# A macaron block on one core: the first tile of each stage turned ahead of the last quarter of the product before it, and the places of the small pieces laid anew

## The chip, the cores and the metric

One Trainium2 chip, one NeuronCore of it. The metric is the device time of one execution in microseconds; lower is better. The numbers given for a kernel are the median of several executions.

## The reference

The input is a 2 x 2048 x 256 float32 tensor, 4096 tokens of 256 values. Three residual blocks follow each other:

```
x = x + 0.5 * moe(layernorm(x))
x = x + recurrence(layernorm(x))
x = x + 0.5 * moe(layernorm(x))

def moe(x):                       # 8 experts, one per token
    probs = softmax(x @ Wr + br); e = argmax(probs)
    h = relu(layernorm_g_b(x) @ W1[e] + b1[e])      # 256 -> 1024
    return (h @ W2[e] + b2[e]) * max(probs)         # 1024 -> 256

def recurrence(x):                # 3 layers of width 64
    x = x @ down.T
    for l in range(3):
        xc = conv4(x) + cb        # causal, 4 taps
        r, i = sigmoid(xc @ Wr[l].T + rb), sigmoid(xc @ Wi[l].T + ib)
        a = exp(8 * r * log_sigmoid(log_a[l]))
        h_t = a_t * h_(t-1) + sqrt(1 - a_t^2) * i_t * xc_t
        x = rms_norm(h @ Wo[l].T) * nw[l]
    return x @ up.T
```

The expert of a token is data: the rows are sorted by expert on the chip.

## The kernel before, in words

**Routing and tiles.** Each of the two expert layers is a pass (pass 0 and pass 1). For a chunk `c` of the tokens (four chunks of 1024 tokens, 512 of each sequence), the router's logits, the choice of the expert, its rank among the rows of that expert and the row's place are computed (`choose`, `place`, `keep_counts` on VectorE, `logits`, `turn_logits`, `ranks`, `counts` on TensorE), and GpSimd (POOL) writes every row into a DRAM table sorted by expert (`route`, L633, two indirect DMAs of 128 rows each time). `tables` on VectorE (six parts) then works out which rows of the table each tile of 128 rows takes and which expert it has; its part 4 raises `s_tab`.

A tile (slot) goes through this chain: SP fetches its 128 rows (`slot_rows`, L465) and the 1 MB first weights of its expert (`slot_weights`, L472), VectorE normalises it (`norm`, L1163), TensorE turns it with two transposes (`turn_input`, L1678), ScalarE applies gain and bias (`affine`, L1417), TensorE multiplies by the first weights (`first_product`, four quarters q of 8 matmuls of 128x128, L1691), ScalarE and VectorE add the bias and clip, a half each (`activate`, L1427 and L1172), TensorE multiplies by the second weights (`second_product`, four quarters of 4 matmuls of 256 columns, L1705), VectorE reads the product and adds the bias (L1181) and finishes the row (L1188, both in `finish`), POOL stores it at its token's place (`store`, L642). 37 tiles are used in each pass; 32 of them in straight code.

**The steady order on TensorE.** In the place of slot i (`fixed_slot`): turn tile i + 1, the four quarters of the first product of tile i, the four quarters of the second product of tile i - 1. `second_product` of tile i waits in its first quarter for both activations and for `m_yk`, VectorE's reading of the product of tile i - 1.

**Stages.** A pass can't begin with all tiles: a tile needs the chunks that its rows come from to be routed. So the tiles come in stages, `FIRST[0] = [0, 9]` and `FIRST[1] = [0, 4, 13, 21]`. Before a stage SP waits (`next_rows`, L481) until the tables of the stage are ready and all rows of its chunks have landed in DRAM, and fetches the first tile only then. On TensorE the turn of the stage's first tile can't stand in the slot before (`next_input` leaves it out), and `begin_stage` (L1723) makes a place of its own for the stage: it turns tile i, then runs the second product of tile i - 1, with pieces of other work between the quarters. After it `fixed_slot` goes on with `next_input`, the turn of tile i + 1, and the first product of tile i. On VectorE `begin_stage` (L1191) does `finish(i - 2)`, the pieces of the place, then `norm(i)` and `norm(i + 1)`; `finish(i - 1)` comes behind these.

**Pieces beside the tiles.** The recurrence, its layernorm and the routing of later chunks are cut into pieces, and every piece of every engine has a number, its place, in the lists at the head of the file. `PLACE[p][i]` is the place of slot i, one more for each stage start before it; `beside(at)` in each engine's block runs the pieces whose number k lies in the stretch `24 * at` to `24 * at + 23`. TensorE has eight such stretches in a place (one behind each quarter), so its place is k / 192; the other engines have two (before and after `activate`, or before and after GpSimd's wait for the half-way point of the first product, `half_through`), so theirs is k / 48. Tile 9 of pass 0 has place 10, its `begin_stage` place 9; in pass 1 tiles 0, 4, 13 and 21 have places 41, 46, 56 and 65, their `begin_stage` the place before. For a chunk c and a layer l of the recurrence the pieces follow in this order: `spread` (PE), `rescale` (DVE), `tap` (ACT), `convolve` (DVE), `gates` (PE), `TANH` (ACT), `gate_input` (DVE), `root` (ACT), `scan` (DVE), `project` (PE), `squares` (ACT), `norms` (PE), `rms_root` (ACT), `inverse` (DVE); each waits on a semaphore of the one before. In front of layer 0 stand the layernorm's moments (DVE), its power (POOL), `transposes` and `logits` (L1548) and `down` (L1585) on TensorE, and `wide` (DVE), which waits for the power.

TensorE also has `in_motion`, matmuls without use before its first real work.

## Time and profile before

| | us |
|---|---|
| median of 3 executions | 715.09 (714.1 to 717.19) |
| the profiled execution, its device time | 712.98 |
| its span, from the first to the last instruction | 711.2 |
| TensorE matmuls busy in it | 657.6 (92%) |
| VectorE busy | 409.6 (58%) |
| ScalarE busy | 272.2 (38%) |
| GpSimd busy | 171.9 (24%) |

Times in the rows below are microseconds from the span's start unless marked ns. PE is TensorE, PEld its weight load, DVE VectorE, ACT ScalarE, POOL GpSimd, SPq the DMA issues of SyncE. A bracket at the end of a row of the timeline is the idle time of the engine before that group and what ended it. Matmul ends are modelled, so that groups which follow each other overlap a little.

### The profile page before, as it was taken

How to read it: one execution, taken by the hardware profiler on the slowest of the kernel's cores; microseconds unless marked ns; L12 is line 12 of the kernel's file. 1: busy time of each engine (PE TensorE's matmuls, PEld its weight loads, DVE VectorE, ACT ScalarE, POOL GpSimd, SP SyncE). 2: the span in 40 equal slices, each digit the busy share in tenths (PEclk: the TensorE clock that was granted, in tenths of full speed). 3: DMA queues.
4: the chain of work that ended last, by engine and by line, in shares of the span. 5: the costliest groups of instructions: out<-in, count | busy, mean ns of one | idle time of the engine just before them, and what ended most of it. 6: DMA issues, size and time to landing. Idle time of an engine off the chain costs nothing.

```text
span 711.2 us, 15531 instructions
## 1 busy us (share of the span) xinstructions
PE 657.6 (92%) x4420; PEld 576.9 (81%) x4420; DVE 409.6 (58%) x1427; ACT 272.2 (38%) x642; POOL 171.9 (24%) x177
## 2 busy tenths in 40 slices
PE   7639997999999999999998989999899989999993
PEld 5429996999988878798777868889689979999992
DVE  7746772333346577776887767787567623333331
ACT  3214221322245557544663436654443223222220
POOL 4733433111121120123302340124212511111111
PEclk9659999999999999999999989999999999999997
DMA  9979673955554463336316345423464466453530
GB/s 281 324 259 396 202 246 109 324 173 193 173 207 142 155 202 117 121 129 217 130 54 238 108 178 208 149 83 120 152 236 141 143 231 207 152 197 101 178 124 14
DMA packets 59920, 126.51 MB, mean 178 GB/s; under 512 B 8106, under 2 KB 36661, under 8 KB 59701
## 3 DMA queue, kind: packets, MB, share of 16 engines
q1 hardware_dynamic: 53204, 108.50, 45.7%
q0 software_dynamic: 6624, 16.92, 6.5%
q8 instruction: 42, 0.69, 0.4%
q14 instruction: 50, 0.40, 0.2%
HBM read 106.36 MB, written 20.35 MB: 178 GB/s over the span
## 4 chain that ended last, share of the span: by engine, by line
PE 70%; DVE 12%; issue 6%; DVEq 5%; DMA 3%; POOL 2%; ACT 1%; POOLq 0%; SPq 0%; ACTq 0%
PE bank L1691 31%; PE bank L1705 29%; PE bank L1678 2%; DVE st L746 2%; POOL routed_rows L633 1%; PE bank L1595 1%; DVEq L400 1%; PE bank L1602 1%; DMA pay<-routed_rows 1%; DVE rec L1082 1%; DVE rec L1058 1%; PE bank L1628 1%; PE bank L1607 1%; PE bank L1533 1%; DVE act_t L1172 1%
## 5 line engine op out<-in xcount | busy, mean ns | idle before, releaser
L1691 PE MATMUL bank<-mn_t,w 128*128 128x128 f32 x2368 | 284.7, 277 | 0.6 <-DVE act_t L1172 0.5
L1691 PEld LDWEIGHTS bank<-mn_t,w 128*128 128x128 f32 x2368 | 275.0, 193 | 9.5 <-issue 7.7
L1705 PE MATMUL bank<-w,act_t 128*128 x1184 | 278.0, 386 | 2.9 <-issue 2.0
L1705 PEld LDWEIGHTS bank<-w,act_t 128*128 128x128 f32 x1184 | 220.7, 193 | 39.5 <-issue 12.8
L1417 ACT ACTIVATE mn_t<-bank,vec 128x128 f32<-128x128 f32 x152 | 61.2, 453 | 236.3 <-PE bank L1678 236.3
L1172 DVE TENSOR_SCALAR act_t<-bank,vec 128x128 f32<-128x128 f32 x296 | 83.3, 344 | 101.9 <-PE bank L1691 88.7
L1427 ACT ACTIVATE act_t<-bank,vec 128x128 f32<-128x128 f32 x296 | 84.6, 368 | 76.0 <-PE bank L1691 75.8
L1181 DVE TENSOR_TENSOR y_b<-bank,b_all 128x256 f32<-128x256 f32 x74 | 31.4, 425 | 104.7 <-PE bank L1705 93.1
L642 POOL DMA_INDIRECT x_middle<-res,pay x37 | 37.2, 1007 | 219.6 <-DVE res L1188 182.7
L642 POOL DMA_INDIRECT out_x<-res,pay x37 | 36.4, 984 | 204.6 <-DVE res L1188 150.2
L633 POOL DMA_INDIRECT routed_rows<-rows,dest x64 | 64.1, 1001 | 53.6 <-PE bank L1691 25.5
L1678 PE MATMUL bank<-ident,mn 128*128 128x128 f32 x152 | 30.4, 282 | 21.6 <-DVE mn L1163 12.8
L1163 DVE TENSOR_SCALAR mn<-pay 128x256 f32<-128x256 f32 x78 | 31.9, 409 | 25.3 <-DMA pay<-routed_rows 24.5
L1678 PEld LDWEIGHTS bank<-ident,mn 128*128 128x128 f32 x152 | 20.5, 145 | 31.6 <-DVE mn L1163 14.2
L625 POOL TENSOR_TENSOR inv_std<-var_eps,minus_half 128x16 f32<-128x16 f32 (+1 forms) x12 | 31.3, 2610 | 51.7 <-DVE var_eps L756 37.3
L1188 DVE SCALAR_TENSOR_TENSOR res<-y_b,pay 128x256 f32<-128x256 f32 x74 | 35.8, 484 | 7.2 <-issue 0.2
L746 DVE BATCH_NORM_STATS2 st<-rows 128x6 f32<-128x256 f32 x96 | 33.7, 414 | 2.6 <-DMA rows<-in_L_attn_h 0.7
L1058 DVE SCALAR_TENSOR_TENSOR rec<-seq,lay,rec 128x512 f32<-128x512 f32 x36 | 27.0, 749 | 2.0 <-issue 0.2
L1321 ACT ACTIVATE xn_t<-bank 128x512 f32<-128x512 f32 x32 | 17.8, 599 | 19.8 <-PE bank L1533 19.6
L1533 PE MATMUL bank<-ident,rows 128*128 128x128 f32 x128 | 20.6, 316 | 0.0
L1533 PEld LDWEIGHTS bank<-ident,rows 128*128 128x128 f32 x128 | 17.7, 166 | 3.1 <-issue 2.2
L1359 ACT ACTIVATE rec<-bank,lay 64x512 f32<-64x512 f32 x24 | 16.4, 682 | 9.0 <-PE bank L1595 8.8
(212 smaller groups left out, 456.5 us busy)
## 6 DMA issues: line engine op xcount, KB each, us to landing
w<-in_L_ffn_W SPq DMA_DIRECT2D x82, 1024.0 KB, 5.2
pay<-routed_rows SPq DMA_DIRECT2D x78, 130.0 KB, 2.1
rows<-in_L_attn_h SPq DMA_DIRECT2D x8, 512.0 KB, 7.2
rows<-x_middle SPq DMA_DIRECT2D x8, 512.0 KB, 5.0
routed_rows<-fill SPq DMA_DIRECT2D x2, 1040.0 KB, 7.7
routed_rows<-rows,dest POOLq DMA_INDIRECT x64, 2.7
b_all<-in_L_ffn_b SPq DMA_DIRECT2D x1, 1024.0 KB, 12.1
x_middle<-res,pay POOLq DMA_INDIRECT x37, 2.5
```

Of the source, the lines that this page charges most:

```text
L633: g.indirect_dma_start(out=routed[f], out_offset=bass.IndirectOffsetOnAxis(ap=dest[:, t:t + 1], axis=0), in_=rows[:, t * RW:(t + 1) * RW], ...
L642: g.indirect_dma_start(out=x_out if p else x_mid, out_offset=bass.IndirectOffsetOnAxis(ap=pay[p][i % RING][:, C_ID:C_ID + 1].bitcast(I32), ...
L746: v.bn_stats(st[:, jj * 6:jj * 6 + 6], tile_of(c, b, j, 0, D))
L1058: last = v.scalar_tensor_tensor(out=r_x_b[cc], in0=seq[:, k:k + CH], scalar=unit(l, k), in1=r_x_b[cc], op0=ALU.mult, op1=ALU.add)
L1172: last = v.tensor_scalar(act_t[i % 2][:, c * P:(c + 1) * P], b_hid[1][:, c % 4 * P:(c % 4 + 1) * P], vec[:, ds(eb + c, 1)], 0.0, ALU.add, ...
L1188: v.scalar_tensor_tensor(out=res[p][i % 2][:, :], in0=y_b[i % 2][:, :], scalar=a[:, C_GATE:C_GATE + 1], in1=a[:, 0:D], op0=ALU.mult, op1=A ...
L1417: last = a.activation(mn_t[p][i % 2][:, k * P:(k + 1) * P], b_in[i % 2][:, k * P:(k + 1) * P], ACT.Identity, scale=vec[:, V_G + k:V_G + k ...
L1427: last = a.activation(act_t[i % 2][:, c * P:(c + 1) * P], b_hid[0][:, c * P:(c + 1) * P], ACT.Relu, bias=vec[:, ds(eb + c, 1)])
L1533: last = t.transpose(bk[cc][n % 2][:, j * P:(j + 1) * P], tile_of(c, b, j, k * P, P), ident[:, :])
L1678: last = t.transpose(b_in[i % 2][:, k * P:(k + 1) * P], mn[p][i % 2][:, k * P:(k + 1) * P], ident[:, :])
L1691: last = t.matmul(b_hid[half][:, c % 4 * P:(c % 4 + 1) * P], w1[i % W1S][:, k * F + c * P:k * F + (c + 1) * P], mn_t[p][i % 2][:, k * P:(k ...
L1705: last = t.matmul(b_out[i % 2], act_t[i % 2][:, c * P:(c + 1) * P], w2[:, ds(eb * (WE // FC) + c * D, D)], start=c == 0, stop=c == FC - 1)
```

## The change

In `begin_stage` of TensorE the wait for the tables and the turn of the stage's first tile move from in front of the whole second product of tile i - 1 to in front of its last quarter (for i = 0 there is no tile before it, and nothing moves). With it the places in the lists were laid anew. GpSimd's lists, LN_POW, R_POW and R_SCATTER, are the same number for number. The places that differ most lie in these stretches: the routing of chunk 3 in pass 0 (choose, ranks, place, counts about half a place to one place earlier), and in pass 1 everything of chunk 3's layernorm and of layers 1 and 2 of chunks 2 and 3 between places 42 and 55.

```diff
--- before.py
+++ after.py
@@ -21,52 +21,52 @@
 
 SUB = 24
 LN_POW = [984, 1272, 1705, 2161]
-LN_WIDE = [1008, 1296, 1704, 2160]
-LN_LOGITS = [4081, 5161, 6865, 8472]
-LN_KEEP_LOGITS = [1033, 1276, 1707, 2136]
-DOWN = [4080, 5162, 6864, 8473]
-KEEP_DOWN = [1032, 1278, 1706, 2160]
-LN_MOMENTS = [[984, 985], [1272, 1273], [1680, 1681], [2114, 2115]]
-LN_TRANSPOSE = [[3984, 4032], [5089, 5113], [6672, 6720], [8257, 8424]]
-LN_KEEP = [[984, 1008], [1273, 1275], [1657, 1704], [2088, 2112]]
-UP = [[5760, 5856], [7057, 7104], [9528, 9600], [11112, 11184]]
-ADD = [[1443, 1465], [1776, 1800], [2380, 2401], [2784, 2786]]
-SPREAD = [[4104, 5163, 6912, 8641], [4656, 5736, 8064, 9504], [5160, 6480, 8880, 10344]]
-RESCALE = [[1032, 1299, 1730, 2209], [1153, 1440, 2016, 2377], [1297, 1632, 2210, 2592]]
-TAP = [[1034, 1320, 1752, 2232], [1176, 1440, 2016, 2379], [1277, 1656, 2233, 2592]]
-CONVOLVE = [[1033, 1300, 1752, 2211], [1176, 1442, 2040, 2378], [1298, 1656, 2256, 2594]]
-GATES = [[4248, 5328, 7056, 9048], [4800, 5832, 8256, 9552], [5232, 6673, 9144, 10488]]
-TANH = [[1080, 1322, 1755, 2280], [1200, 1464, 2064, 2381], [1321, 1658, 2281, 2640]]
-GATE_INPUT = [[1080, 1344, 1778, 2281], [1224, 1489, 2113, 2425], [1320, 1705, 2304, 2688]]
-ROOT = [[1104, 1368, 1920, 2328], [1224, 1512, 2137, 2448], [1392, 1705, 2329, 2712]]
-SCAN = [[1104, 1392, 1824, 2328], [1248, 1560, 2116, 2520], [1416, 1729, 2352, 2736]]
-PROJECT = [[4560, 5664, 7392, 9432], [5088, 6336, 8616, 10224], [5713, 6960, 9481, 11040]]
-SQUARES = [[1128, 1416, 1921, 2376], [1272, 1608, 2161, 2544], [1418, 1753, 2378, 2760]]
-NORMS = [[4608, 5712, 7440, 9480], [5112, 6384, 8640, 10272], [5737, 7008, 9505, 11088]]
-RMS_ROOT = [[1152, 1417, 1922, 2377], [1274, 1609, 2162, 2568], [1419, 1754, 2380, 2761]]
-INVERSE = [[1152, 1417, 1969, 2376], [1274, 1608, 2208, 2570], [1441, 1753, 2379, 2760]]
+LN_WIDE = [1008, 1297, 1704, 2161]
+LN_LOGITS = [4081, 5161, 6865, 8424]
+LN_KEEP_LOGITS = [1033, 1276, 1707, 2112]
+DOWN = [4080, 5162, 6864, 8425]
+KEEP_DOWN = [1032, 1278, 1706, 2114]
+LN_MOMENTS = [[984, 985], [1272, 1273], [1680, 1681], [2065, 2137]]
+LN_TRANSPOSE = [[3984, 4032], [5089, 5113], [6672, 6720], [8232, 8257]]
+LN_KEEP = [[984, 1008], [1273, 1275], [1657, 1704], [2040, 2088]]
+UP = [[5760, 5856], [7057, 7104], [9482, 9504], [11112, 11184]]
+ADD = [[1443, 1465], [1776, 1800], [2377, 2381], [2784, 2786]]
+SPREAD = [[4104, 5163, 6912, 8689], [4656, 5736, 8064, 9505], [5160, 6480, 8688, 10416]]
+RESCALE = [[1032, 1299, 1730, 2208], [1153, 1440, 2016, 2380], [1296, 1632, 2162, 2592]]
+TAP = [[1034, 1320, 1752, 2208], [1176, 1440, 2016, 2380], [1277, 1656, 2162, 2640]]
+CONVOLVE = [[1033, 1300, 1752, 2256], [1176, 1442, 2041, 2401], [1298, 1656, 2209, 2616]]
+GATES = [[4248, 5328, 7056, 9096], [4800, 5832, 8256, 9720], [5208, 6673, 9024, 10560]]
+TANH = [[1080, 1322, 1755, 2280], [1200, 1464, 2064, 2424], [1321, 1658, 2256, 2641]]
+GATE_INPUT = [[1080, 1344, 1778, 2304], [1224, 1489, 2088, 2448], [1320, 1705, 2280, 2688]]
+ROOT = [[1104, 1368, 1920, 2329], [1224, 1512, 2113, 2472], [1392, 1705, 2328, 2712]]
+SCAN = [[1104, 1392, 1824, 2352], [1248, 1560, 2114, 2497], [1416, 1729, 2328, 2736]]
+PROJECT = [[4560, 5664, 7392, 9481], [5088, 6336, 8520, 10104], [5713, 6960, 9432, 11040]]
+SQUARES = [[1128, 1416, 1921, 2378], [1272, 1608, 2160, 2544], [1418, 1753, 2376, 2760]]
+NORMS = [[4608, 5712, 7440, 9483], [5112, 6384, 8568, 10224], [5737, 7008, 9480, 11088]]
+RMS_ROOT = [[1152, 1417, 1922, 2379], [1274, 1609, 2161, 2568], [1419, 1754, 2377, 2761]]
+INVERSE = [[1152, 1417, 1969, 2378], [1274, 1608, 2160, 2570], [1441, 1753, 2376, 2760]]
 R_POW = [[None, None, 0, 48], [1512, 1848, 2424, 2808]]
-R_CHOOSE = [[None, None, 3, 96], [1512, 1968, 2448, 2832]]
-R_EXP = [[None, None, 49, 120], [1560, 1992, 2472, 2856]]
-R_RANKS = [[None, None, 216, 552], [6192, 7944, 9936, 11472]]
-R_PLACE = [[None, None, 48, 144], [1536, 2017, 2472, 2856]]
-R_COUNTS = [[None, None, 288, 696], [6288, 8160, 10008, 11544]]
-R_KEEP_COUNTS = [[None, None, 73, 168], [1561, 2041, 2496, 2880]]
+R_CHOOSE = [[None, None, 2, 72], [1512, 1968, 2424, 2832]]
+R_EXP = [[None, None, 48, 96], [1560, 1992, 2425, 2856]]
+R_RANKS = [[None, None, 193, 408], [6192, 7944, 9816, 11472]]
+R_PLACE = [[None, None, 48, 96], [1536, 2017, 2472, 2856]]
+R_COUNTS = [[None, None, 264, 504], [6288, 8160, 9984, 11544]]
+R_KEEP_COUNTS = [[None, None, 50, 121], [1561, 2040, 2496, 2880]]
 R1_TRANSPOSE = [0, 48]
-R1_KEEP = [1, 24]
+R1_KEEP = [0, 24]
 R1_LOGITS = 192
-R1_KEEP_LOGITS = 48
-R_TURN_LOGITS = [[None, None, None, 217], [5952, 7368, 9696, 11256]]
-R_MOMENTS = [[[None, None], [None, None], [None, None], [1, 2]], [[1464, 1488], [1777, 1825], [2400, 2424], [2785,
+R1_KEEP_LOGITS = 49
+R_TURN_LOGITS = [[None, None, None, 216], [5952, 7368, 9600, 11256]]
+R_MOMENTS = [[[None, None], [None, None], [None, None], [0, 1]], [[1464, 1488], [1777, 1825], [2379, 2400], [2785,
     2808]]]
 R_SCATTER = [[[None, None, None, None], [None, None, None, None], [72, 120, 168, 216], [264, 312, 360, 408]],
     [[1560, 1608, 1656, 1704], [2040, 2088, 2136, 2160], [2472, 2520, 2568, 2616], [2856, 2904, 2952, 3000]]]
-TABLE_PARTS = [[[None, None, None, None, None, None], [169, 192, 240, 264, 288, None]], [[1584, 1609, 1633, 1682,
-    1683, 1728], [2064, 2065, 2088, 2089, 2112, 2280], [2497, 2544, 2568, 2569, 2593, 2616], [2881, 2904, 2905,
+TABLE_PARTS = [[[None, None, None, None, None, None], [168, 216, 217, 264, 312, None]], [[1584, 1609, 1633, 1682,
+    1683, 1728], [2064, 2066, 2112, 2113, 2115, 2136], [2520, 2521, 2544, 2545, 2568, 2569], [2881, 2904, 2905,
     2952, 2953, None]]]
-LAYER_COLUMNS = 0
-EXP_LOG_A = 0
-LOG_SIGMOID = 72
+LAYER_COLUMNS = 49
+EXP_LOG_A = 72
+LOG_SIGMOID = 120
 
 
 
@@ -1723,11 +1723,16 @@
             def begin_stage(p, i):
 
                 beside(8 * (PLACE[p][i] - 1))
-                pe.wait_ge(s_tab, tables_at(p, FIRST[p].index(i)))
-                turn_input(p, i)
-                if i:
+                if i == 0:
+                    pe.wait_ge(s_tab, tables_at(p, 0))
+                    turn_input(p, i)
+                else:
                     eb = second_expert(p, i - 1)
                     for q in range(4):
+                        if q == 3:
+
+                            pe.wait_ge(s_tab, tables_at(p, FIRST[p].index(i)))
+                            turn_input(p, i)
                         second_product(p, i - 1, q, eb)
                         beside(8 * (PLACE[p][i] - 1) + 1 + q)
 
```

## Rows read from the trace of the kernel before

**Rows 1.** The page: busy time (share) and instructions; one group of part 5.

```profile
PE 657.6 (92%) x4420; PEld 576.9 (81%) x4420; DVE 409.6 (58%) x1427; ACT 272.2 (38%) x642; POOL 171.9 (24%) x177
...
L1058 DVE SCALAR_TENSOR_TENSOR rec<-seq,lay,rec 128x512 f32<-128x512 f32 x36 | 27.0, 749 | 2.0 <-issue 0.2
```

**Rows 2.** TensorE's waits over the span: us in total, times, longest.

```profile
PE bank L1678 <- DVE mn L1163: 12.8, 2, 11.2
PE bank L1678 <- issue: 6.7, 3, 3.3
...
PE bank L1602 <- DVE rec L1082: 2.0, 4, 0.7
...
PE bank L1595 <- DVE rec L1058: 1.5, 3, 0.6
```

**Rows 3.** Timeline around tile 9 of pass 0: start, us, engine, line, operation.

```profile
114.68 3.62 PE L1705 MATMUL bank<-w,act_t 128*128 x16
...
115.25 0.97 POOL L633 DMA_INDIRECT routed_rows<-rows,dest  x1 [0.30 <-issue]
...
121.14 0.34 SPq L465 DMA_DIRECT2D pay<-routed_rows  x1
...
121.56 0.41 PE L1678 MATMUL bank<-ident,mn 128*128 128x128 f32 x2 [3.26 <-issue]
...
122.72 5.40 PE L1705 MATMUL bank<-w,act_t 128*128 x16 [0.75 <-issue]
...
126.02 0.41 DVE L1163 TENSOR_SCALAR mn<-pay 128x256 f32<-128x256 f32 x1 [4.49 <-DMA pay<-routed_rows]
...
128.18 2.06 PE L1691 MATMUL bank<-mn_t,w 128*128 128x128 f32 x17
```

**Rows 4.** Stretches: window, us, PE busy (groups), granted clock, DMA share, GB/s.

```profile
123.00:128.00 5.00, 5.00 (x17) 0.66 1.02 409
420.00:428.00 8.00, 7.79 (x28) 0.57 0.97 361
576.00:581.00 5.00, 2.96 (x14) 1.00 1.03 392
```

**Rows 5.** Timeline around tile 4 of pass 1.

```profile
406.96 1.95 PE L1691 MATMUL bank<-mn_t,w 128*128 128x128 f32 x16
...
408.84 1.07 PE L1548 MATMUL bank<-xn_t,wr_c 128*32 128x512 f32 x8
...
409.83 1.94 PE L1585 MATMUL bank<-xn_t,down_t 128*64 128x512 f32 x8
...
414.11 0.97 POOL L633 DMA_INDIRECT routed_rows<-rows,dest  x1 [0.30 <-issue]
...
415.89 2.04 POOL L625 TENSOR_TENSOR inv_std<-var_eps,minus_half 128x8 f32<-128x8 f32 x1 [0.81 <-DVE var_eps L754]
...
417.49 0.35 SPq L465 DMA_DIRECT2D pay<-routed_rows  x1
...
420.21 1.51 PE L1607 MATMUL bank<-half_sel,rec 128*128 128x2 f32 x8 [1.26 <-ACT rec L1374]
...
422.89 5.87 PE L1705 MATMUL bank<-w,act_t 128*128 x16
...
424.10 0.41 DVE L1163 TENSOR_SCALAR mn<-pay 128x256 f32<-128x256 f32 x1 [2.38 <-DMA pay<-routed_rows]
...
428.82 2.84 PE L1691 MATMUL bank<-mn_t,w 128*128 128x128 f32 x24
```

**Rows 6.** Timeline around tile 13 of pass 1.

```profile
508.99 0.42 DVE L1181 TENSOR_TENSOR y_b<-bank,b_all 128x256 f32<-128x256 f32 x1 [1.15 <-PE bank L1705]
...
514.17 0.41 DVE L1163 TENSOR_SCALAR mn<-pay 128x256 f32<-128x256 f32 x1 [3.72 <-DMA pay<-routed_rows]
...
515.06 3.74 PE L1691 MATMUL bank<-mn_t,w 128*128 128x128 f32 x32
```

**Rows 7.** Timeline around tile 21 of pass 1.

```profile
578.74 0.41 PE L1678 MATMUL bank<-ident,mn 128*128 128x128 f32 x2 [1.57 <-issue]
...
579.25 0.81 ACT L1417 ACTIVATE mn_t<-bank,vec 128x128 f32<-128x128 f32 x2 [6.06 <-PE bank L1678]
...
583.38 3.74 PE L1691 MATMUL bank<-mn_t,w 128*128 128x128 f32 x32
```

## The prediction, made before the changed kernel was run

> **What bounds the kernel now.** I read the page first: TensorE is busy for 92% of the span [rows 1], so what can be won is its idle time and its slow clock. Then its waits: outside the loading of the first tiles, nearly all idle time stands in front of one line, L1678, the turning of an input tile; the waits that the recurrence pieces cause are small beside it, 2.0 us for the projections and 1.5 us for the gates over the whole kernel [rows 2]. Of L1678's waits, the 12.8 us are those of the very first tile and of tile 0 of the second pass, which the new `begin_stage` handles as the old did. The change can reach the four other stage starts: tile 9 of pass 0 and tiles 4, 13 and 21 of pass 1. For each I read the timeline of all engines, and asked two things: when the first tile of the stage is normalised (that releases the turn), and when the second is, because `next_input` turns the second tile before the first tile's first product may start. That second tile is the one a plain reading of the diff forgets.
>
> **Pass 0, tile 9.** The product in front (tile 7's, L1705 at 114.68 for 3.62 us) ends at 118.30. The last routed rows were issued at 115.25, the tile could be fetched only when they had landed, and the turn comes at 121.56 after 3.26 us of idling, and only then tile 8's 16 matmuls run, at 122.72 for 5.40 us; the first product of tile 9 starts at 128.18 [rows 3]. After the change 12 of those 16 fill the wait. They can't start at 118.30: `second_product` waits until VectorE has read the product before it, and at a stage start that reading begins 0.46 us after the product's end and takes 0.42 us (at tile 13 product 11 ends at 508.53 and the reading starts at 508.99 [rows 6]), so about 119.2. Twelve matmuls at 0.217 us (16 in about 3.5 us) end at 121.8, the turn takes 0.2, the last four 0.9: 122.9. But tile 10, fetched at 121.14, is normalised at 126.02 to 126.43, because its rows and 1 MB of weights come over the same queue [rows 3]. TensorE waits again, from 122.9 to 126.5, and starts the first product at 126.8 for 128.18: 1.4 us won, not 3.3.
>
> The clock takes it back. In the trace the granted clock falls after the wait: 0.66 on average in 123 to 128, which is 0.34 x 5 / 0.5 = 3.4 us at half of 2.4 GHz, the other of its two levels being 1.2; a stretch without a fall, 576 to 581, has 1.00 [rows 4]. It cost half of 3.4, 1.7 us, of which a part was free since tile 10 was late anyway. After the change 3.6 us of idling lie in one piece, directly in front of slots in which nothing waits, and I expect the same fall there, now paid in full: +1.7. Sum of this start: -1.4 + 1.7 = +0.3 us. Its bounds: -1.4 if the clock holds, +2.0 if it falls twice.
>
> **Pass 1, tile 4.** Here most of the re-placed pieces meet. In the old order logits and down projection of chunk 3 (408.84 to 411.77, 2.9 us) stand inside tile 3's first product; projection and norms of layer 1, chunk 2 stand behind tile 2's second product, where TensorE waits 1.26 us for ScalarE until 420.21; the clock is low for 0.43 x 8 / 0.5 = 6.9 us [rows 4], and tile 3's 16 matmuls take 5.87 us. First product of tile 4: 428.82 [rows 5]. In the new order logits and down stand before tile 3's first product, project behind its last quarter (PROJECT 8616 to 8520), norms inside tile 2's second product (8640 to 8568). Take H as the moment when tile 3's first product is half through: 408.75 before (406.96 with 1.95 us, less the overlap), and 2.9 us later after. POOL's list is not changed in one number, so its last four row DMAs still wait for H, at 0.97 and a gap of 0.30 us each (the last began at 414.11, SP went on at 417.49 [rows 5], 2.4 us after that one's end). Before, a store was in their way; after, the later H leaves the store in front. So SP fetches tile 4 at H + 0.1 + 5.0 + 2.4 = H + 7.5. Tile 5 was normalised 6.6 us behind that fetch, at 424.10 [rows 5], plus 0.41: H + 14.6. TensorE's own chain: first product's rest 1.8 (as its first half), second product 3.5, wait for the read 0.9, twelve matmuls 2.6, and project, norms and the pair of spreads (the layer-2 spread stands here now) at 1 us each, my estimate from the norms' 1.51 us in the low clock, 3.0: H + 11.8, turn of tile 4, last quarter until H + 12.9, wait for tile 5 until 14.6, first product at H + 14.9. Against 428.82 = old H + 20.1, and with H 2.9 later and 0.5 us of spread brought forward: 20.1 - 14.9 - 2.9 + 0.5 = 2.8, and I take -2.7. Covers: VectorE does inverse, wide and rescale before it normalises tile 4; at no more than the 0.75 us each of its costliest 128x512 form [rows 1] these are 2.2 us, beside eight matmuls and two spreads; if that cover is gone, the turn is late by up to 1 us, but tile 5's wait hides it. Table part 5, moved from behind the stage's start to before it, adds seven short instructions to VectorE in the same cover. Bounds: -4.4 (tile 5 as soon as TensorE is free) to +0.7 (the 3.4 us of low clock, twice 1.7, come back).
>
> **Pass 1, tile 13.** Product 11 is read at 508.99 + 0.42, tile 14 normalised at 514.17 to 514.58, first product at 515.06 [rows 6]. The second tile again binds: 0.2 us. The layer-2 spread of chunk 3 now stands behind the half-way point that releases POOL, so the rows come 0.5 us earlier against TensorE's work: together -0.7. The gates of chunk 3 now stand before product 12 and wait for a convolution that begins after tile 12's activation; TensorE then idles some 0.3 us there, which the 1.8 us wait for tile 14 would have taken anyway: nothing. If the clock falls, +1.7: bounds -0.7 and +1.0.
>
> **Pass 1, tile 21.** The rows are there; TensorE waited 1.57 us for VectorE to finish product 19 first [rows 7]. After: start at 577.17 + 0.9 = 578.05, twelve matmuls to 580.65; turn, affine of ScalarE ready 1.3 us after the turn's start (578.74 to 579.25 + 0.81 [rows 7]), so tile 22 is turned at 582.0 and the first product starts at 582.3 for 583.38: -1.1. The price of the change, the affine that now hides behind four matmuls instead of sixteen, is in it: 0.5 us. Bounds -1.2 and -0.6.
>
> **All other places.** The pieces of early chunk 3 (routing of pass 0) and of the recurrence move, but each is issued once as before. What they can win is the 3.5 us of [rows 2] at most, of which little lies outside tile 4's stage; what they can lose is of the same size. I take 0, bounds -1.5 and +2.
>
> **Sum.** +0.3 - 2.7 - 0.7 - 1.1 = -4.2 us. Against the profiled execution's own 712.98 us that is 708.8. That execution was 2.1 us faster than the median of the runs shown, 715.09, so 710.9 us is my number for the median.
>
> A rule against the change stands in the Trainium skill, "TensorE: Matmul & The Clock Gate", section "HAM oscillation — how this bites in real kernels": short bursts of matmuls between DMA waits make the clock fall again at every burst. This trace agrees in part: it fell at tile 9 after one wait of 3.26 us, but also at tile 4 where no single wait was over 1.3 us [rows 5], and not at tile 21 after 1.57 us [rows 4, 7].
>
> **The rivals.** (A) The waits only move and the clock falls there: the second tile binds at tiles 4, 9 and 13, and each new wait (3.6, 1.7, 1.8 us in one piece) is followed by a half-clock stretch. For it: tile 9. Against: at tile 21 1.57 us did no harm. Price: 1.7 us at each of tiles 4 and 13 over the forecast, -0.8 us in all: 714.3. By the skill's rule it would be this one. Chance 0.32. (B) Slower: VectorE's queue at tile 4. Tile 4 is normalised only behind inverse, wide and rescale, wide needs POOL's power after the four row DMAs, rescale needs TensorE's spread between the quarters. If the power is late, TensorE stands in the spread, then in the turn, and then in tile 5. It decides once the power ends over 2.5 us after product 3 could have started; with both waits and two clock stretches that is 3 to 6 us instead of -2.7, and with A's falls the kernel ends near 719. Against it: POOL's power took 2.04 us from 415.89 [rows 5] and was over before tile 4's turn even in the old order. Chance 0.08. (C) All of it: the clock holds at tile 9 too and the re-placed pieces save 1 to 2 us: 707.5 to 709.5. Chance 0.15. (D) The change doesn't do what it says, because the first tile was never last: that is true of tile 21 alone, where the gain is VectorE's order, and is in the sum.
>
> **Numbers.** Forecast 0.45 (709.5 to 712.5), A 0.32, C 0.15, B 0.08. A measurement of this kernel can tell about 0.5%, 3.6 us, from no change. Under 711.5: all of C and two thirds of the forecast, 0.45 with rounding; A, the rest of the forecast and some of B are no change, 0.47; slower 0.08. The range leaves out half of C's low end and B: 708.0 to 715.0.
>
> **What would show it.** Right: L1678's idle time falls from four waits to waits in front of the second tiles, ended by tile rows; 12 L1705 matmuls directly before each first turn, 4 behind; tile 9's first product about 8.5 us after product 7's end; the wait at L1607 gone; one low stretch near 125 and none near 421. Wrong: idle time at L1595, L1602 or L1617 above 5 us, or low stretches at tiles 4 and 13 (A), or a wait of over 2 us in front of tile 4's turn (B).

## The result and the profile after

The changed kernel takes 718.44 us (median of 20 executions, 714.53 to 721.34) against 715.12 us for the kernel before (20 executions, 713.3 to 718.26): a ratio of 1.0039 by all executions, 95% interval 1.0025 to 1.0052 (the quotient of the two medians is 1.0046). It is 0.4% slower. The forecast was 710.9 us with a range of 708.0 to 715.0; the result lies outside it. The profiled execution took 719.86 us with a span of 718.1, 1.4 us over its median, while the one before lay 2.1 us under its own. So the two spans differ by 6.9 us, of which about half is the choice of executions. One correction to the counts ahead of this section: a float32 matmul of the code stands as two records in the trace (the first product issues 16 and has 32 records), so where the kernel's description and the prediction count the matmuls of a product or of a quarter (16, 12, 8 or 4), these are records (a transpose stands as one); the times are not touched by that, and what follows counts records.

The page, and TensorE's waits (us in total, times, longest), which answer to [rows 1, 2]:

```profile
PE 662.8 (92%) x4420; PEld 580.7 (81%) x4420; DVE 409.8 (57%) x1427; ACT 270.1 (38%) x640; POOL 172.8 (24%) x177
```

```profile
PE bank L1678 <- DVE mn L1163: 8.2, 4, 3.1
PE bank L1705 <- DVE y_b L1181: 6.4, 6, 2.2
...
PE bank L1691 <- ACT act_t L1427: 1.9, 1, 1.9
```

The waits `L1678 <- issue`, 6.7 us before, are gone: the first tile of a stage no longer keeps TensorE waiting. In their place stand the normalising of the second tile, VectorE's reading of a product (L1705, up to 2.2 us) and a wait for ScalarE's activation that was not there. Of the 8.2 us of normalising, 1.6 us in front of tile 1 of pass 1 were there before; the new ones are 3.10 us at tile 10, 3.15 us at tile 14 and 0.39 us at tile 5. The 11.2 us of the very first tile [rows 2] stand at another line in this profile, so the totals of this group can't be compared.

The timeline of the changed kernel in pass 0 (start, us, engine, line, operation), which answers to [rows 3]:

```profile
75.66 0.16 DVE L1023 TENSOR_SCALAR logs<-logs 128x3 f32<-128x3 f32 x1
...
79.91 0.42 DVE L1181 TENSOR_TENSOR y_b<-bank,b_all 128x256 f32<-128x256 f32 x1 [0.82 <-issue]
...
80.58 3.72 PE L1705 MATMUL bank<-w,act_t 128*128 x16 [0.90 <-DVE y_b L1181]
...
89.30 0.21 DVE L917 TENSOR_TENSOR_SCAN seg_end<-seg_n,zero_e 128x32 f32<-128x32 f32 x1
...
95.48 0.42 DVE L1181 TENSOR_TENSOR y_b<-bank,b_all 128x256 f32<-128x256 f32 x1
...
117.77 3.62 PE L1705 MATMUL bank<-w,act_t 128*128 x16
...
122.21 2.85 PE L1705 MATMUL bank<-w,act_t 128*128 x12 [0.82 <-DVE y_b L1181]
...
128.77 0.41 DVE L1163 TENSOR_SCALAR mn<-pay 128x256 f32<-128x256 f32 x1 [4.50 <-DMA pay<-routed_rows]
...
129.24 0.44 PE L1678 MATMUL bank<-ident,mn 128*128 128x128 f32 x2 [3.10 <-DVE mn L1163]
...
129.52 5.37 PE L1691 MATMUL bank<-mn_t,w 128*128 128x128 f32 x32
```

And in pass 1, around tiles 3, 4 and 5, then tile 13 ([rows 5, 6]):

```profile
415.18 3.84 PE L1691 MATMUL bank<-mn_t,w 128*128 128x128 f32 x32
...
423.04 1.41 DVE L746 BATCH_NORM_STATS2 st<-rows 128x6 f32<-128x256 f32 x4
...
425.74 0.42 DVE L1181 TENSOR_TENSOR y_b<-bank,b_all 128x256 f32<-128x256 f32 x1 [0.59 <-issue]
...
426.41 3.40 PE L1705 MATMUL bank<-w,act_t 128*128 x8 [2.18 <-DVE y_b L1181]
...
433.61 3.74 PE L1691 MATMUL bank<-mn_t,w 128*128 128x128 f32 x32
...
436.10 0.41 DVE L1163 TENSOR_SCALAR mn<-pay 128x256 f32<-128x256 f32 x1 [1.46 <-DMA pay<-routed_rows]
...
436.50 0.68 DVE L1103 TENSOR_TENSOR seq<-rec,bank 128x512 f32<-128x512 f32 x1
...
437.22 0.82 ACT L1350 ACTIVATE rec<-seq,lay 128x512 f32<-128x512 f32 x1 [2.59 <-DVE seq L1103]
...
438.17 1.15 ACT L1427 ACTIVATE act_t<-bank,vec 128x128 f32<-128x128 f32 x4
...
439.46 1.13 PE L1691 MATMUL bank<-mn_t,w 128*128 128x128 f32 x8 [1.89 <-ACT act_t L1427]
...
508.46 0.48 DVE L1188 SCALAR_TENSOR_TENSOR res<-y_b,pay 128x256 f32<-128x256 f32 x1
...
509.22 0.97 POOL L642 DMA_INDIRECT out_x<-res,pay  x1 [4.28 <-DVE res L1188]
...
510.50 0.98 POOL L633 DMA_INDIRECT routed_rows<-rows,dest  x1 [0.31 <-issue]
...
515.48 0.34 SPq L465 DMA_DIRECT2D pay<-routed_rows  x1
...
522.40 0.69 PE L1678 MATMUL bank<-ident,mn 128*128 128x128 f32 x2 [3.15 <-DVE mn L1163]
...
522.89 5.13 PE L1691 MATMUL bank<-mn_t,w 128*128 128x128 f32 x32
```

Stretches of the changed kernel with a low clock around its stages (window, us, PE busy, granted clock, DMA share, GB/s), which answer to [rows 4]:

```profile
125.00:134.00 9.00, 5.90 (x35) 0.81 1.00 398
388.00:395.00 7.00, 6.28 (x43) 0.76 0.48 144
426.00:431.00 5.00, 4.59 (x17) 0.66 0.77 267
437.00:446.00 9.00, 7.11 (x49) 0.81 0.46 156
522.00:528.00 6.00, 5.59 (x36) 0.72 0.88 343
```

**Where the time went.** I took from each timeline the start of every tile's first product (the L1691 group; other line numbers in the experiments) and subtracted. "1.4" is tile 4 of pass 1. The row `e9` belongs to a kernel described below.

| us from ... to ... | before | after | e1 | e2 | e3 | e9 |
|---|---|---|---|---|---|---|
| span's start to 0.8 | 111.1 | 114.2 | 111.0 | 114.0 | 111.2 | 111.1 |
| 0.8 to 0.10 (start of the stage of tile 9) | 20.9 | 20.7 | 20.6 | 21.3 | 20.8 | 16.2 |
| 0.10 to 1.0 | 253.4 | 254.0 | 253.3 | 253.3 | 254.0 | 254.1 |
| 1.0 to 1.1 | 3.9 | 5.5 | 5.5 | 3.9 | 5.4 | 5.2 |
| 1.1 to 1.4 | 39.6 | 39.1 | 38.7 | 39.6 | 39.0 | 38.4 |
| 1.4 to 1.6 | 14.6 | 17.2 | 14.6 | 14.6 | 17.2 | 14.6 |
| 1.6 to 1.20 (with tile 13) | 126.5 | 127.2 | 126.7 | 126.3 | 127.0 | 126.3 |
| 1.20 to 1.21 | 13.4 | 12.4 | 12.4 | 13.4 | 12.4 | 12.4 |
| 1.21 to the end | 127.8 | 127.8 | 127.8 | 127.8 | 127.8 | 127.8 |
| span | 711.2 | 718.1 | 710.5 | 714.2 | 714.6 | 705.9 |

What was aimed at moved little: tile 9 -0.1, tile 4 -0.5, tile 21 -1.0. Three places that I had priced at nothing lost more: the routing in pass 0 (+3.1), the stretch behind tile 4 (+2.5) and 1.0 to 1.1 (+1.6).

Each column is one profiled execution, and some rows move by themselves. Thirteen profiles of this document have the old places of pass 0 and the same code until tile 8; they take 111.0 to 113.5 us for it, 111.9 in the mean. Above that mean the changed kernel and e2 (114.2 and 114.0) lie by 2.1 to 2.3 us, not by 3.1. The stretch 1.4 to 1.6 has a spread as well: the changed kernel and e3 take 17.2 us there, but e5, e6, e11 and e14, whose pieces in front of tile 4's activation are the same, 14.9 to 15.4. So the sizes are taken from the ratios of many executions below, and the rows say where.

### The profile page after: what moved, and what is told of

Same layout as the page of the kernel before. It is cut to its first block, busy times and chain, and to the rows that moved or that the text cites. A ratio compares the mean times of both kernels' runs of the same rounds, so it can differ in the third digit from the quotient of the medians.

```text
span 718.1 us, 15529 instructions
## 1 busy us (share of the span) xinstructions
PE 662.8 (92%) x4420; PEld 580.7 (81%) x4420; DVE 409.8 (57%) x1427; ACT 270.1 (38%) x640; POOL 172.8 (24%) x177
## 4 chain that ended last, share of the span: by engine, by line
PE 71%; issue 7%; DMA 6%; DVE 5%; POOL 2%; another core or an unknown queue 2%; DVEq 2%; SPq 1%; ACT 1%; POOLq 0%; ACTq 0%
PE bank L1691 31%; PE bank L1705 27%; DMA pay<-routed_rows 4%; PE bank L1678 2%; PE bank L1533 2%; POOL routed_rows L633 2%; PE bank L1595 2%; PE bank L1602 1%; DMA routed_rows<-rows,dest 1%; DVE st L746 1%; PE bank L1628 1%; PE bank L1607 1%; PE bank L1585 1%; PE bank L1561 1%
## 5 line engine op out<-in xcount | busy, mean ns | idle before, releaser
L1691 PE MATMUL bank<-mn_t,w 128*128 128x128 f32 x2368 | 289.3, 280 | 2.2 <-ACT act_t L1427 1.9
L1691 PEld LDWEIGHTS bank<-mn_t,w 128*128 128x128 f32 x2368 | 279.7, 196 | 10.5 <-issue 10.3
L1705 PE MATMUL bank<-w,act_t 128*128 x1184 | 275.7, 383 | 6.6 <-DVE y_b L1181 6.4
L1705 PEld LDWEIGHTS bank<-w,act_t 128*128 128x128 f32 x1184 | 218.4, 191 | 43.3 <-issue 17.5
L1678 PE MATMUL bank<-ident,mn 128*128 128x128 f32 x152 | 30.4, 283 | 10.6 <-DVE mn L1163 8.2
L1678 PEld LDWEIGHTS bank<-ident,mn 128*128 128x128 f32 x152 | 20.3, 145 | 21.2 <-DVE mn L1163 10.5
L1561 PEld LDWEIGHTS bank<-pick,lg_t 128*128 128x128 f32 x64 | 9.1, 217 | 14.3 <-ACT lg_t L1330 14.0
L1533 PE MATMUL bank<-ident,rows 128*128 128x128 f32 x128 | 20.6, 313 | 0.0
L1561 PE MATMUL bank<-pick,lg_t 128*128 128x16 f32 x64 | 9.2, 278 | 12.3 <-ACT lg_t L1330 12.3
```

The costliest lines, as they stand in the source:

```text
L1533: last = t.transpose(bk[cc][n % 2][:, j * P:(j + 1) * P], tile_of(c, b, j, k * P, P), ident[:, :])
L1678: last = t.transpose(b_in[i % 2][:, k * P:(k + 1) * P], mn[p][i % 2][:, k * P:(k + 1) * P], ident[:, :])
L1691: last = t.matmul(b_hid[half][:, c % 4 * P:(c % 4 + 1) * P], w1[i % W1S][:, k * F + c * P:k * F + (c + 1) * P], mn_t[p][i % 2][:, k * P:(k ...
L1705: last = t.matmul(b_out[i % 2], act_t[i % 2][:, c * P:(c + 1) * P], w2[:, ds(eb * (WE // FC) + c * D, D)], start=c == 0, stop=c == FC - 1)
```

## The experiments

The theory when they were planned: the turn itself wins, and the new numbers in the lists lose more. The rival: the turn loses, by waits and clock falls at the second tiles (A of the prediction). The kernels of one group shared their runs of the kernel before, whose medians were 716.24 (e1 to e4), 715.18 (e5 to e8), 715.66 (e9 to e12) and 716.77 us (e13 to e15). The lines of the experiments are shifted: the turn L1678, the first product L1691, the second L1705 and SP's fetch L465 stand at L1674, L1687, L1701 and L461, in e7, e9 and e15 at L1683, L1696, L1710 and L461.

### e1, e2, e3 and e12: the change in halves

e1 has the new `begin_stage` and every old place; e12 is e1 again, in another group.

```diff
-                pe.wait_ge(s_tab, tables_at(p, FIRST[p].index(i)))
-                turn_input(p, i)
-                if i:
+                if i == 0:
...
+                        if q == 3:
+                            pe.wait_ge(s_tab, tables_at(p, FIRST[p].index(i)))
+                            turn_input(p, i)
```

> The new begin_stage with every place of the kernel before. Theory P (the places): the turn itself wins and the new places lose. It should be 1 to 3 us faster than before (712 to 714 against 715.1), tile 21 by about 1.0 us as in the changed kernel; tile 9 and tile 13 near nothing, because their second tile binds. Theory T (the turn): the longer waits in front of the second tiles cost clock; it should be 1 to 3 us slower than before (716 to 718), as slow as the changed kernel within 1 us.

> The same kernel as the run with the turn alone, to have it on the same chip beside the others of this group. 1 to 3 us faster than before again (ratio 0.995 to 0.999).

Measured: e1 713.3 us, 0.997 [0.995, 0.9991]; e12 713.26 us, 0.9977 [0.9957, 0.9996]. The turn alone makes the kernel faster, by 2.1 and 1.6 us; the rival falls.

e2 has the old `begin_stage` with the new numbers of what runs in pass 0:

```diff
-R_CHOOSE = [[None, None, 3, 96], ...
+R_CHOOSE = [[None, None, 2, 72], ...
-TABLE_PARTS = [[..., [169, 192, 240, 264, 288, None]], ...
+TABLE_PARTS = [[..., [168, 216, 217, 264, 312, None]], ...
-LOG_SIGMOID = 72
+LOG_SIGMOID = 120
...
```

> The old begin_stage, and of the new places only those of pass 0's routing and of the start (choose, place, ranks, counts and tables of chunks 2 and 3, the layer columns and the log-sigmoid). Theory P: TensorE waits 0.8 to 0.9 us twice before tile 9 for VectorE's reading of a product (L1181), which stands behind the log-sigmoid and behind table parts 1 and 2; 1.7 to 2.0 us slower than before (about 717). Theory T: no difference, within 0.5 us of before.

e3 is the changed kernel with these numbers old, so that only the new places of the recurrence and of pass 1 are left beside the turn.

> The changed kernel with the old places for pass 0's routing and the start; the recurrence's places and those of pass 1 stay new. Theory P: the two waits at L1181 before tile 9 are gone and it is 1.7 to 2.0 us faster than the changed kernel, 716.0 to 716.7. If the places of pass 1 lose as well, it is still slower than the run with the turn alone by the wait of about 2 us for L1181 in front of tile 3's second product and the 1.9 us for tile 5's activation. Theory T: like the changed kernel, 718.

Measured: e2 717.35 us, 1.0034 [1.0012, 1.0056]; e3 716.04 us, 1.0001 [0.9981, 1.0021]. The parts add up: turn -0.27% (mean of e1 and e12), pass 0's places +0.34%, the recurrence's places +0.28% (e3 less that mean) give +0.35%, and +0.39% was measured. The first two are shown; the third is a difference whose interval, an estimate from those given, is 0.25% to either side and nearly reaches zero. Its largest row in the table, +2.5 us at 1.4 to 1.6, stands in e3 and in the changed kernel and not in e1 or e2.

### e5 and e14: which piece of pass 0

e5 is the changed kernel with `LAYER_COLUMNS`, `EXP_LOG_A`, `LOG_SIGMOID` and the parts of the tables in pass 0 as before. e14 is the same with one number more:

```diff
-LOG_SIGMOID = 72
+LOG_SIGMOID = 144
```

> The changed kernel with two of its lists put back: the layer columns, the exponential and the log-sigmoid, and pass 0's table parts; chunk 3's choose, ranks, place and counts stay at the new places. If those two lists alone cause the two waits at L1181 before tile 9, it is as fast as the run with all of pass 0's old places (716.0), 1.7 to 2.4 us faster than the changed kernel, and the waits for L1181 before tile 9's stage are gone. If the loss is spread over the routing, it gains less than 1 us.

> The changed kernel with pass 0's table parts and the layer columns at their old places, and the log-sigmoid at 144, a place where no other piece of VectorE stands beside it; chunk 3's routing stays new. Theory: the loss of pass 0 comes from two heaps on VectorE in front of its reading of a product (the log-sigmoid with the counts, table parts 1 and 2 together), and with both apart tile 0 to tile 8 takes 60 to 61.5 us, not 63.5; ratio 1.000 to 1.002 against the changed kernel's 1.0039. Rival (chunk 3's earlier routing itself costs): it stays at 1.0035 or more.

e5 missed: 718.99 us, 1.0052 [1.0033, 1.0071]. The two waits for y_b are gone, but the log-sigmoid at its old number 72 meets `choose`, whose new number is 72 as well, and TensorE's sums wait for it:

```profile
73.95 0.21 PE L1568 MATMUL bank<-chosen,tri 128*128 128x64 bf16 x1 [2.76 <-DVE sums L827]
```

The mixture had a fault of its own and so told nothing. e14 takes both away: 716.29 us, 0.9992 [0.997, 1.0014], 0.5% below the changed kernel's ratio. The time fits, the rows only in part: tile 0 to tile 8 takes 63.3 us in its profile, where 60 to 61.5 was expected and the changed kernel has 63.5. In it the waits of 0.90 and 0.82 us are down to none and to 0.19 and 0.51 us at other products, but one wait of 1.52 us stands in front of tile 1's second quarter, at 58.69. That one doesn't come from these places: it is 0.34 us in the changed kernel, and 1.06 to 1.82 us at the same place in e4, e6, e11, e13 and e15, which have the old places of pass 0. Why it comes and goes was not settled.

### e13: one number

e3 with the tap of layer 0, chunk 3, behind tile 4's activation again:

```diff
-TAP = [[1034, 1320, 1752, 2208], ...
+TAP = [[1034, 1320, 1752, 2232], ...
```

> The changed kernel with pass 0's places old, and one number more put back: TAP of layer 0, chunk 3, from 2208 (before ScalarE's activation of tile 4) to 2232 (behind it). Theory: in the changed kernel ScalarE stands in that tap, which waits for VectorE's rescale, which waits behind the normalising of tile 6 for its rows; so tile 4's activation is late, TensorE waits 1.9 us before tile 5's first product and the clock falls. With the number back the wait is gone and it is 1.9 to 3.6 us faster than the 716.0 us (ratio 1.000) without it: 712.5 to 714.2, ratio 0.995 to 0.998. Rival (the loss of pass 1 is made at tile 13): no difference, ratio 0.9985 or more.

713.88 us, 0.9969 [0.9949, 0.9988], 2.3 us less than e3 by the ratios. ScalarE now activates first and taps behind it, and 1.4 to 1.5 takes 3.8 us, not 5.8:

```profile
431.77 3.74 PE L1687 MATMUL bank<-mn_t,w 128*128 128x128 f32 x32
...
433.86 1.15 ACT L1423 ACTIVATE act_t<-bank,vec 128x128 f32<-128x128 f32 x4 [1.08 <-PE bank L1687]
...
435.03 0.81 ACT L1346 ACTIVATE rec<-seq,lay 128x512 f32<-128x512 f32 x1
```

One number of the 112 that changed, on an engine that is busy for 38% of the span, held about as much as all of the recurrence's places lose. The two intervals overlap a little (0.9949 to 0.9988, 0.9981 to 1.0021), so the size is uncertain. The rows show the wait: TensorE waits 1.2 to 1.9 us for tile 4's activation in all six profiles with the tap in front (the changed kernel, e3, e5, e6, e11, e14), and not in e13. What they don't show is that this wait always costs 2.3 us. Behind it the clock fell in the changed kernel and in e3 alone (17.2 us from 1.4 to 1.6); in the other four it held, and they take 14.9 to 15.4 us, beside 14.9 in e13, where a wait of 1.05 us for VectorE stands in front of the gates instead. In e6:

```profile
435.50 1.13 PE L1687 MATMUL bank<-mn_t,w 128*128 128x128 f32 x8 [1.21 <-ACT act_t L1423]
...
437.58 2.94 PE L1687 MATMUL bank<-mn_t,w 128*128 128x128 f32 x24
```

### e6: the tables of tile 13

e3 with the six parts of the tables in front of tile 13 as before:

```diff
-    [2520, 2521, 2544, 2545, 2568, 2569]
+    [2497, 2544, 2568, 2569, 2593, 2616]
```

> The changed kernel with pass 0's places old and, of pass 1, the six table parts of tile 13's stage at their old places. Theory: parts 4 and 5 now stand before VectorE's finish of tile 10, POOL's store of tile 10 waits for that and the last row DMAs of the stage for POOL, so tile 13's rows come 2 us later. With the parts back, SP fetches tile 13 at 5.8 to 6.3 us after the half of tile 12's first product instead of 7.9, and the time falls by 1.5 to 3 us from 716.0 to 713 to 714.5. If POOL's delay has another cause, it stays within 0.7 us of 716.0.

716.49 us, 1.0016 [0.9994, 1.0037]: no gain. The rows did come earlier, since SP fetches 6.9 us behind the half of the first product and not 8.0 (5.8 to 6.3 was expected), but two other waits appeared with a low clock behind them:

```profile
509.89 1.09 PE L1591 MATMUL bank<-rec,rec_t 64*64 64x512 f32 x8 [2.01 <-DVE rec L1054]
...
513.06 5.48 PE L1701 MATMUL bank<-w,act_t 128*128 x12 [2.08 <-DVE y_b L1177]
```

### e11: half of the recurrence back

e3 with layers 1 and 2 of chunk 3 and the routing of chunks 2 and 3 as before.

> The changed kernel with pass 0's places old, and of pass 1 the new ones only up to about place 49 (chunk 3's layernorm, layer 1 of chunk 2, layer 2 of chunk 2, layer 0 of chunk 3); layers 1 and 2 of chunk 3 and the routing of chunks 2 and 3 stand at the old places. Theory: the loss of pass 1 is made around tile 13, where the gates of chunk 3 stand ahead of product 12 and the rows come late; then this is as fast as the turn alone (within 0.7 us). If it is made around tiles 4 and 5, it is 1.5 to 2.5 us slower than the turn alone.

723.53 us, 1.0112 [1.0083, 1.0142]. From 1.6 to 1.8 it takes 30.9 us where all others take 21.2 to 21.7: old and new numbers crossed there (its longest new wait is 4.7 us, the gates' for VectorE). It separates nothing; what it shows is that numbers of these lists can't be mixed freely.

### e4: turn the second tile later

e1 with `next_input` at the three later stage starts behind the second quarter of the first product:

```diff
+                    if late and q == 1:
+                        next_input(p, i + 1)
```

> The turn alone (old places), and at each stage start after the first the turn of the second tile moved from in front of the first tile's first product to behind that product's second quarter. If the second tile is what binds (its rows 3 to 4 us later), the waits of about 3 us in front of L1678 at tiles 9 and 13 fall to what the weights of the first tile need, and it is 2 to 5 us faster than the turn alone. If the weights or the clock bind instead, it is within 0.7 us of the turn alone.

713.57 us, 0.9966 [0.9947, 0.9985], the same as e1. The wait only went from the rows of tile 10 to the first weights of tile 9:

```profile
126.50 2.02 PE L1687 MATMUL bank<-mn_t,w 128*128 128x128 f32 x16 [2.03 <-issue]
```

So the plain reading of [rows 3], that tile 10's rows bind, was incomplete: weights and rows are issued in turn by SP, and the weights are there only some 1 us before the rows are normalised (3.1 us of waiting in e1, 2.0 here).

### e8 and e10: keep TensorE in motion through the wait

e1 with matmuls without use in front of tile 10's turn, 12 in e10 and 24 in e8.

```diff
+                    if (p, i) == (0, 9):
+                        in_motion(12)
```

> The turn alone with 24 matmuls without use (128 columns, into the bank whose contents have been read) in the 3.1 us wait in front of the second tile of stage 9. Theory of the clock: the wait drops the clock and costs 1.7 us of the following first product; with the wait filled the first product of tile 9 takes 3.6 to 3.8 us instead of 5.0 and the kernel is 1.2 to 1.7 us faster than the turn alone. If the low stretch comes from something else (the loads, the stage itself), no difference, or up to 0.5 us slower from the filling.

> The turn alone with 12 matmuls without use in the wait in front of tile 10's turn, instead of the 24 that took 5.5 us for a wait of 3.1 us and so cost 2.4 us more than they hid. Theory of the clock: 12 take 2.7 us and fit in the wait, tile 9's first product takes 3.7 us and not 5.0, and it is 1.0 to 1.7 us faster than the turn alone. Otherwise no difference.

e8: 715.54 us, 1.0001 [0.9986, 1.0017], 2.0 us slower than e1 and e12 by the ratios, where 1.2 to 1.7 us faster was expected. I had sized it wrongly: 24 of them are 48 records and took 5.52 us, for a wait of 3.1. The first product behind them took 3.74 us, so 0.8 to 0.10 takes 21.1 us against 20.6 in e1 and e12; where the rest of the 2.0 us went was not settled. e10 with half of them fits in the wait:

```profile
123.01 2.84 PE L1666 MATMUL bank<-ident 128*128 128x128 f32 x24
...
126.24 0.44 PE L1674 MATMUL bank<-ident,mn 128*128 128x128 f32 x2 [0.40 <-DVE mn L1159]
...
126.52 3.74 PE L1687 MATMUL bank<-mn_t,w 128*128 128x128 f32 x32
```

The first product behind it takes 3.74 us, and 5.0 and 5.1 in e1 and e12: with the wait filled, the clock holds in both profiles. 712.65 us, 0.9968 [0.9949, 0.9986], 0.6 us less than e12, which is not resolved; 1.0 to 1.7 was expected. And the clock can hold without filling too. Nine profiles have the unfilled wait of 3.0 to 3.2 us in front of tile 10's turn; in eight the clock falls behind it, and in e6, which has the same code there as e3 and e13, it doesn't:

```profile
128.50 0.44 PE L1674 MATMUL bank<-ident,mn 128*128 128x128 f32 x2 [3.02 <-DVE mn L1159]
128.78 3.74 PE L1687 MATMUL bank<-mn_t,w 128*128 128x128 f32 x32
```

That the filling is what kept the clock up is therefore likely (eight falls in nine profiles without it, none in two with it), but not shown.

### e7, e9 and e15: the weights ahead of the rows

SP doesn't need the routed rows to load the first weights of a stage, only the tables. e9 is e1 with the weights of the stage's first two tiles issued before the wait for the rows, and left out at their old place (e7: of its first three):

```diff
+                if i in FIRST[p][1:]:
+                    for k in range(2):
+                        next_weights(p, i + k)
```

> The turn alone (old places), and SP issues the first weights of the three first tiles of each later stage before it waits for the stage's rows, instead of between the rows. Theory: the second tile's rows come 4 to 5 us after their fetch only because they share the queues with megabytes of weights. Then tiles 10 and 14 are normalised 2 to 3 us earlier, the wait of 3.1 us in front of tile 10's turn falls under 1 us, the clock no longer falls at tile 9, and it is 3 to 6 us faster than the turn alone (707 to 710). If the rows themselves or SP's issue are the limit, under 1 us.

> The turn alone (old places), and SP issues the first weights of only the first two tiles of each later stage before it waits for the stage's rows; in the run with three, the third megabyte was issued at the same time as the last row DMAs of POOL, whose rows landed 5.9 us after their issue instead of 2.6. Theory (contention): with two the loads are over before those row DMAs, SP fetches tile 9 0.6 us after product 7's end as in the turn alone, tile 10's rows come 2 to 3 us earlier than there, and it is 2 to 5 us faster than the turn alone. If the rows of the second tile are late for another reason, or the clock falls all the same, within 1 us of it.

e7: 717.25 us, 1.0017 [0.9992, 1.0041]; 707 to 710 was expected. Three loads of 1 MB are one too many: the third was issued at 117.6, while POOL scattered the last rows, and these came late:

```profile
117.17 0.97 POOL L638 DMA_INDIRECT routed_rows<-rows,dest  x1 [0.30 <-issue]
...
124.03 4.02 SPq L461 DMA_DIRECT2D pay<-routed_rows  x4
...
126.59 0.41 PE L1683 MATMUL bank<-ident,mn 128*128 128x128 f32 x2 [2.70 <-issue]
```

From the end of the last row DMA's issue (118.14) to SP's fetch it takes 5.9 us, where the changed kernel has 2.3 (119.32 to 121.65) and no load was issued in the 7 us before. The Trainium skill, "DMA: Bandwidth & Descriptors", section "Issuing engines are not separate DMA queues", has the rule: transfers share the same 16 DMA engines and interleave, whichever engine started them. The trace agrees, by these 5.9 against 2.3 us.

e9, with two: **708.12 us** (707.34 to 710.91), 0.9908 [0.9881, 0.9936], faster than both kernels, 1% below the one before. Its profile at tile 9:

```profile
118.50 2.54 SPq L461 DMA_DIRECT2D pay<-routed_rows  x3
...
121.62 0.41 DVE L1168 TENSOR_SCALAR mn<-pay 128x256 f32<-128x256 f32 x1 [0.53 <-DMA pay<-routed_rows]
...
123.44 3.74 PE L1696 MATMUL bank<-mn_t,w 128*128 128x128 f32 x32
```

Three tiles' rows are fetched one after the other with nothing between them, the second is normalised 1.0 us behind the first (120.61 to 121.62) instead of 5.0 (123.79 to 128.77 in the changed kernel), the wait of 3.1 us is gone and the clock holds: 16.2 us from 0.8 to 0.10, not 20.6. At this tile the loads were issued before 108.4 and the last rows took 2.3 us to SP's fetch; at tiles 4 and 13 two loads still run beside the last rows, and these take 6.0 and 6.2 us. So nearly all that e9 wins over e1, 4.4 of 4.6 us between the two profiles, is won at tile 9.

e15 asks whether this belongs to the turn or stands alone: e9's SP with the old `begin_stage`.

> The two early megabytes of the fastest run, but the old begin_stage (turn in front of the whole product) and all old places. It says what the turn is worth when the second tile is not late. Theory: the turn won only 2 us because the second tile's rows bound; with those early it wins 0.8 to 2.0 us at each of tiles 9, 4 and 13 and 1.0 at tile 21, so this run is 3.5 to 6 us slower than the run with both (708.1, ratio 0.9908): ratio 0.996 to 0.999. Rival (the early weights do it all): within 2 us of it, ratio under 0.9935.

722.58 us, 1.0084 [1.0051, 1.0116]. Alone, the early weights are a loss; with them the turn is worth 1.0084 less 0.9908, 12.6 us, where 3.5 to 6 was expected. By the profiles 4.9 us of it are in the stage of tile 9 (21.1 us from 0.8 to 0.10), 4.9 at tile 13, 3.0 at tile 4 and 2.6 at tile 21. Tile 13:

```profile
508.45 1.53 SPq L468 DMA_DIRECT2D w<-in_L_ffn_W  x2
...
509.27 1.17 POOL L638 DMA_INDIRECT routed_rows<-rows,dest  x1 [0.30 <-issue]
...
516.52 2.54 SPq L461 DMA_DIRECT2D pay<-routed_rows  x3
519.31 0.66 PE L1683 MATMUL bank<-ident,mn 128*128 128x128 f32 x2 [5.66 <-issue]
...
520.23 5.74 PE L1710 MATMUL bank<-w,act_t 128*128 x16 [0.25 <-issue]
```

The weights meet POOL's rows here as well, and SP's fetch comes 6.1 us behind the last one (510.44 to 516.52). In the old order TensorE waits for that in one piece, 5.66 us, and then runs 16 records at a low clock. In e9 the same delay (501.35 to 507.53, 6.2 us) lies under 12 records and leaves a wait of 1.53 us.

## Why the prediction was wrong

**The step that failed** is "All other places: I take 0, bounds -1.5 and +2". The new places cost +0.34% in pass 0 (2.4 us, e2) and about 0.28% in the recurrence (2.0 us, e3 against e1 and e12), 4.4 us together, over twice the upper bound. (The second holds also what the new places did inside the stages of tiles 4 and 13.) The turn alone won 1.9 us where the sum had 4.2 for the four stages; -1.9 and +4.4 give +2.5 us, and the ratio says +2.8. I had taken the idle time of the pieces in the old trace [rows 2] as the size of what could be lost. That bounds only what can be won; a piece in a new place can make a wait where there was none, and there it also delays the tile chain. What I left out was to walk VectorE's and ScalarE's lists for each moved number and ask which tile instruction now stands behind it:

- Pass 0: fifteen short instructions of the log-sigmoid (75.66 to 79.0) stand ahead of the reading of a product at 79.91, and two parts of the tables (89.30 to 95.4) ahead of the one at 95.48. TensorE waits 0.90 and 0.82 us at the products behind them. e14, with both heaps apart, is faster by 3.4 us by the ratios. The rows carry the first heap: from tile 3 to tile 4 it takes 8.4 us in the changed kernel and 8.3 in e2, 7.2 to 7.4 in the fifteen other profiles. They don't settle the second: from tile 5 to tile 6 it takes 8.3 and 8.5 us in these two, but also 8.0 in e14 and 8.0 to 8.8 in e4, e6, e7 and e8, which have the old places.
- Pass 1: the tap of chunk 3 stands ahead of tile 4's activation on ScalarE. It waits for VectorE's rescale, which stands behind the normalising of tile 6, which waits 1.46 us for its rows. So a 0.8 us piece ties ScalarE to a DMA, the activation begins at 438.17 instead of some 435.7 (in e13 it follows its first product's start by 2.09 us), TensorE waits 1.89 us, and the clock is at 0.81 in 437 to 446. e13 shows the wait, by taking it away; that the clock falls behind it was seen in two of six profiles.

**Tile 9** (forecast +0.3, measured -0.1, in e1 -0.3). The steps held: the first product of tile 9 starts 8.1 us after product 7's end (121.39 to 129.52) instead of 9.9, forecast 8.5; tile 10 binds with a wait of 3.10 us, forecast 3.6; and the fall of the clock takes 1.6 us back (the product takes 5.37 us, not 3.74), forecast 1.7. e9 shows the first half by taking its cause away. For the second, that the wait brings the fall, e8 and e10 speak, but in e6 the clock held behind the same wait.

**Tile 4** (forecast -2.7, measured -0.5 from 1.1 to 1.4, -0.9 in e1). With H = 417.0 the fetch came at H + 8.1 (forecast 7.5), but the first product at H + 16.6 (forecast 14.9). The sum had 0.9 us for the wait at 426.41, which took 2.18: VectorE works out the moments of the next chunk (423.04) before it reads product 2 (425.74), and the eight records behind the wait take 3.40 us at half clock. I had counted VectorE's moved work only against the normalising of tile 4, not against the reading that `second_product` waits for. The wait at L1607 went, as forecast, and a longer one took its place. The low stretch near 421 went, and one at 426 to 431 (0.66) took its place. Of the four terms of the sum this one was off the most, by 2.2 us.

**Tile 13** (forecast -0.7; 1.6 to 1.20 measured +0.7, in e1 +0.2). "The rows come 0.5 us earlier" was wrong. POOL's list has no new number, but its times changed: its last two row DMAs stand behind the store of product 10 (509.22), which waits for VectorE's finish (508.46), and that stands behind parts of the tables. The fetch came 7.9 us behind the half of the first product, tile 14 bound with 3.15 us, and the product behind it took 5.13 us. e6 brought the fetch forward by 1.1 us and lost the gain elsewhere, so what this one is worth alone stays open.

**Tile 21** (forecast -1.1, measured -1.0, in e1 too): right.

**1.0 to 1.1** (forecast 0, measured +1.6): the clock falls after two waits of 1.60 and 1.05 us; in the profile before, waits of 1.61 and 1.05 us stand at the same place and the clock holds (3.74 us). Of the profiles here only those of the kernel before and of e2 lack the fall; e15, which has the old `begin_stage`, shows it, so it isn't tied to the turn. Its cause is open.

**The rivals.** A's mechanism, waits at second tiles with a fall of the clock behind them, is what happened at tiles 9 and 13 of the changed kernel; at tile 4 the second tile's wait was 0.39 us and no fall stood behind it (433.61, 3.74 us). The rule of the Trainium skill named there, "TensorE: Matmul & The Clock Gate", section "HAM oscillation — how this bites in real kernels", agrees with the rows of tiles 9 and 13 (5.37 and 5.13 us), not with e6 at tile 9 (3.02 us of waiting, then 3.74). A's number for the whole, 714.3, lies near the 713.3 us of e1, but that is luck: e1 waits 3.06 us at tile 10 with a fall, and at tile 14 only 1.27 us with none (3.74 us). A had left out the places as well. B had the right sign and the right engine, VectorE's queue at tile 4, but the wrong instruction: the reading of a product and then ScalarE's tap, not the wide and rescale in front of the turn; and half of the loss was in pass 0, where no rival looked. A chance of 0.08 for slower was too low for a change with 112 new numbers, of which I priced about ten.

## What to carry to other kernels

When a static order is laid anew, price every moved piece by what now stands behind it on its own in-order engine, and follow what that piece itself waits for: a 0.8 us piece that waits for a DMA at third hand kept TensorE waiting for 1.2 to 1.9 us in every profile that had it there. The idle time of a class of pieces in the old trace bounds what moving them can win, never what it can lose. A wait that is shortened at one tile shows the next transfer in the queue; here the gain came only when the order of the loads was changed with it (0.9908), and that order of loads was a loss without the turn (1.0084): measure two such edits together as well as apart.
